# A graph layer's first tile: its products eight tiles behind x instead of six, three adjacency tiles requested later, and the first expert's weights requested behind x

## The chip, the cores and the metric

The kernel runs on one core of a Trainium2 chip. The metric is the device time of one execution in microseconds. Where several runs are shown, the median counts.

## What is computed

Two layers follow each other on x, 4096 tokens of 256 features, with adj a 4096 x 4096 adjacency of zeros and ones. The first is a graph convolution with residual, the second a mixture of 16 experts of which each token uses 2.

```python
deg = jnp.maximum((adj != 0).astype(jnp.float32).sum(-1), 1.0)
# graph layer on layernorm(x):
dinv = jax.lax.rsqrt(node_degree)
a_norm = dinv * (adjacency + jnp.eye(n)) * dinv
pooled = a_norm @ x + x
x = x_in + relu(pooled @ W + b)
# expert layer on layernorm(x), for e in range(16), top 2 of softmax(x @ Wr + br):
h = jax.nn.gelu(xf @ W1[e] + b1[e], approximate=False)
y = y + combine[:, e:e + 1] * (h @ W2[e] + b2[e])
x = x + xf + y
```

## The kernel before

Rows of x and of the adjacency are handled in 32 tiles of 128. The kernel has two halves.

**The graph half.** It does not compute a_norm @ x and then times W, but first y = layernorm(x) @ W for all 32 tiles of x and then the adjacency times y. y is kept in two float16 parts, a high half `yh` and a low half `yl` (inside the large buffer `wall`), so each product of an adjacency block with y is a pair of matmuls: L502 with the high half, L504 with the low half. An adjacency tile is 128 rows of the adjacency. It arrives as float16 in four quarters (`load_adj`, L255, into one of four slots of `abuf`), VectorE adds the identity (`add_own`, L876), transposes it in four chunks (`transpose_chunk`, L884) into `at`, and the TensorE products of a chunk wait for its transpose (`at_made`). An adjacency tile has 32 pairs, eight to a chunk.

The first stage, `first_tile` (L542 to L563), makes y and multiplies the first adjacency tile in the same loop. For each tile n of x:

- TensorE transposes x (`x_T`, L530) and multiplies tile n - 1 by W (`x_times_W`, L538). From n = LAG on, which is 6, it also multiplies adjacency block j = n - LAG (`neighbours`), after a wait for the chunk at every eighth j and for `y_low` of tile j. Ahead of the first of them stands one small product (L554). The loop runs until n = 32 + LAG - 1, so behind the last x times W come LAG pairs, of which the first stands in the same pass.
- ScalarE copies x transposed out of PSUM (`copy_x_T`, L749) and makes the high half of y (`high_y`, L756), scaled by the rstd of the token.
- VectorE makes the low half (`low_y`, L891) and the statistics of x six tiles ahead (`stats_of`, L844). When a group of tiles (`GROUPS`: 0-1, 2-4, 5-7, then four tiles each) is complete, five small instructions make its variance (L851 to L860). After the low half of tiles 4, 10, 18 and 26 (L907) it also transposes chunk 0, 1, 2 or 3 of adjacency tile 0, the first time after adding the identity.
- POOL makes rstd of each group (L1298), which waits for the variance. Behind groups 2, 4 and 6 it issues the four requests for adjacency tile 1, 2 or 3 (L1301). Those of tile 0 are issued earlier, from 5.57 us on.
- SP issues the requests for the larger part of x (L366 to L375), without waiting. ScalarE issues the others at the start.

Behind it `step` (L565 for TensorE, L395 for SP, L1047 for VectorE) runs for each adjacency tile t from 1 to 31, with what makes layer one's result, the router's choice and the rows for the experts, one and two tiles behind. SP's step 0 waits for the small `b2_cut` of VectorE, which comes when the x loop is over, then writes b2's low part, pads, and asks for the first matrix of expert 0 (L412, into `wst`); step 2 asks for the second one after it has stored a tile of the base. ScalarE (`cut_high_weights`, L694) and VectorE (`cut_low_weights`, L959) split them into two float16 parts. The weights of experts 1 to 7 follow in the loop in the same way, behind waits on `w_cut`.

**The expert half.** 79 blocks of 128 rows, each of one expert: transposes (L602), hidden products (L628), bias and gelu, transposes (L636), output products (L654), weighting, and an indirect DMA that adds the rows to the output (L1370). Between the halves stands a stretch in which the table of blocks is made.

The order on each engine is as written in the code. There is no scheduler.

Of the kernel before, what the change touches and what calls it, by code (L numbers as in the profile page):

```python
# [48 lines left out]
JC = CW // P  # L49
AB = 4  # L50
DEPTH = 2
LAG = 6
GROUPS = ((0, 2), (2, 5), (5, 8)) + tuple((n, n + 4) for n in range(8, 32, 4))
LEAD = 6
SG = 2.0 ** 8
# [11 lines left out]
XT = T // XC  # L67
# [20 lines left out]
def build(nc, x, adj, gnn_W, gnn_b, Wr, br, W1, b1, W2, b2, out):  # L88
# [5 lines left out]
    def sem(name):  # L94
        return ctx.enter_context(nc.semaphore(name))
# [119 lines left out]
    def ev(name):  # L215
        if name not in S:
            S[name] = sem(name)
        return S[name]

    def after(eng, name, t):  # L220

        eng.wait_ge(ev(name), t + 1)

    def passed(eng):


        eng.sem_inc(ev("passed"), 1)
# [5 lines left out]
    w_in = [sem(f"w_in{k}") for k in range(2)]  # L233
# [7 lines left out]
    def after_added(eng, q, r):  # L241

        n = q * (U // 2) + r // 2
        eng.wait_ge(added[r % 2], (n + 1) * 16)
# [8 lines left out]
    def load_adj(eng, i, k, b):  # L253

        eng.dma_start(arrived[b * PQ:(b + 1) * PQ, k % AB, :, :],  # L255
                      adj_v[bass.ds(pair(i, k), 1), k % 2, b, :, :, :].rearrange("n i a c -> i (n a) c"))\
           .then_inc(a_in[k % AB], 16)

    def load_x(eng, c, b):
        first, end = PIECES[c], PIECES[c + 1]  # L260
        eng.dma_start(xin[b * PQ:(b + 1) * PQ, first:end, :].rearrange("p (n h) d -> p n (h d)", h=2),
                      x_v[b][:, first // 2:end // 2, :]).then_inc(x_in[c], 16)
# [11 lines left out]
    def tile(i, k):  # L274

        return i * RUN + k

    def pair(i, k):

        return i * (RUN // 2) + k // 2  # L280
# [5 lines left out]
    def over_tiles(eng, step):  # L286

        for k in range(RUN):
            step(0, k)
        with eng.Fori(1, T // RUN - 1) as i:  # L290
            for k in range(RUN):
                step(i, k)
        for k in range(RUN + DEPTH):
            step(T // RUN - 1, k)

    def asked_at(i):

        return (0, 1) if isinstance(i, int) and i == T // RUN - 1 else (0, 2)
# [5 lines left out]
    def is_(t, cond):  # L304

        return cond(t) if isinstance(t, int) else True
# [16 lines left out]
    def w_dram(e, which):  # L323
        return (W1, W2)[which][bass.ds(e, 1), :, :].rearrange("a (c p) n -> p (a c) n", p=P)

    def staged(slot, which):
        return wst[:, slot, :].rearrange("p (c n) -> p c n", c=(DC, HC)[which])
# [10 lines left out]
    def fixed(q):  # L338

        return isinstance(q, int) and q == 0  # L340
# [21 lines left out]
    @block.sync  # L362
    def _(sp):
        sp.dma_start(wg_arrival, gnn_W.rearrange("(c p) n -> p c n", p=P)).then_inc(ev("w_gnn_in"), 16)
        for b in QUEUE[0]:
            load_x(sp, 0, b)  # L366
        for b in QUEUE[0]:
            load_x(sp, 1, b)
        for b in QUEUE[0]:
            load_x(sp, 2, b)  # L370
        for dst, src in consts:
            sp.dma_start(dst, src).then_inc(ev("consts_in"), 16)
        for c in (3, 4):
            for b in (0, 2, 1, 3):
                load_x(sp, c, b)  # L375

        def store_base(i, k):
            after(sp, "base_made", tile(i, k))
            sp.dma_start(out_v[bass.ds(pair(i, k), 1), k % 2, :, :, :].rearrange("n a i d -> (n a) i d"), base[k % 2])\
              .then_inc(base_out[k % 2], 16)  # L380

        def load_late(j):

            sp.wait_ge(ev("w_cut"), 2 * EARLY + (j - 1 if j >= 2 else 0))
            sp.dma_start(staged(j % 2, j % 2), w_dram(EARLY + j // 2, j % 2)).then_inc(w_late[j % 2], 16)

        b1_v = b1.rearrange("(c e) h -> c (e h)", c=CH).unsqueeze(1)

        def load_b1(c):

            sp.wait_ge(ev("at_made"), (T - AB + c + 1) * CH)
            n = E * H // CH
            sp.dma_start(b1all[:, c * n:(c + 1) * n], b1_v[c].broadcast_to([P, n])).then_inc(ev("b1_in"), 16)

        def step(i, k):  # L395
            t = tile(i, k)
            if is_(t, lambda t: 2 <= t < T + 2):
                store_base(i, k - 2)
            if isinstance(t, int) and T - 2 <= t < T:
                load_b1(t - T + 2)  # L400
            if isinstance(t, int) and t == 0:
                sp.wait_ge(ev("b2_cut"), 1)
                after(sp, "b2_zeros", 0)
                sp.dma_start(b2hl[E:2 * E, :], b2l).then_inc(ev("b2_in"), 16)
                after(sp, "pad_made", 0)
                sp.dma_start(rows[0:U * ROOM, :].rearrange("(e r) w -> r e w", r=ROOM)[0:P, :, :],
                             pad[:, :].unsqueeze(1).broadcast_to([P, U, RW])).then_inc(ev("first_pads"), 16)
            if k in asked_at(i):
                which = asked_at(i).index(k)
                if is_(i, lambda i: i >= 1):  # L410
                    sp.wait_ge(ev("w_cut"), i * 2 + which - 1)
                sp.dma_start(staged(which, which), w_dram(i, which)).then_inc(w_in[which], 16)  # L412
            if isinstance(t, int) and t == T - 1:
                load_late(0)
                load_late(1)

        over_tiles(sp, step)

        def load_block(q, r):
            if not isinstance(q, int) or q > 0:  # L420
                after_added(sp, q - 1, r)
            if fixed(q):
                row = r * ROOM
            else:
                passed(sp)
                row = sp.value_load(tab[0:1, bass.ds(in_table(q, r), 1)], min_val=0, max_val=PLACES - P)
            sp.dma_start(xg[r], rows[bass.ds(row, P), :]).then_inc(xg_in[r], 16)

        AHEAD = 4

        def bstep(q, r):
            nxt = shift(q, r, AHEAD)
            if is_block(nxt, 1, 0):
                after(sp, "table_made", 0)
                sp.wait_ge(ev("spare_pads"), 16)
                for which in range(len(PADS)):
                    after_pads(sp, which)
            if exists(*nxt):
                load_block(*nxt)
            if late(q, r) is not None and r % 2 and late(q, r) + 2 < 2 * (E - EARLY):  # L440
                load_late(late(q, r) + 2)

        for odd in (0, 1):
            sp.wait_ge(listed[odd], 16 * TOPK * T // 2)
        sp.wait_ge(ev("multiplied"), T * CH)
        for r in range(AHEAD):
            load_block(0, r)
        load_b1(2)
        load_b1(3)
        over_blocks(sp, bstep)  # L450


        for b in (BLOCKS - 2, BLOCKS - 1):
            after_added(sp, *divmod(b, U))
# [3 lines left out]
    def _(pe):  # L458
# [83 lines left out]
        def first_tile():  # L542

            for n in range(T + LAG):
                if n < T:
# [3 lines left out]
                if 0 <= n - 1 < T:  # L549
                    x_times_W(n - 1)  # L550
                j = n - LAG
                if j == 0:
# [279 lines left out]
    def _(dve):  # L832
# [45 lines left out]
        def transpose_chunk(i, k, c):  # L878

            n = tile(i, k) * CH + c  # L880
            after(V, "own_added", tile(i, k))
            if is_(n, lambda n: n >= CH):
                V.wait_ge(ev("multiplied"), n - CH + 1)
            V.transpose(at[:, c, :].bitcast(I32).rearrange("p (n a i) -> p a n i", a=Q, i=PQ),  # L884
                        arrived[:, k % AB, :, c * CW // CH:(c + 1) * CW // CH].bitcast(I32)
                        .rearrange("p a (n q) -> p a n q", q=PQ))\
             .then_inc(ev("at_made"), 1)
# [15 lines left out]
        for n in range(T):  # L903
            low_y(n)
            if n + LEAD < T:
                stats_up_to(n + LEAD)
            if n in (XT // 2, XT + 2, 2 * XT + 2, 3 * XT + 2):  # L907
                if n < XT:
                    add_own(0, 0)
                transpose_chunk(0, 0, n // XT)  # L910
            if n == T // 4 + 2:
                after(V, "gb_high", 0)
                V.scalar_tensor_tensor(out=gbm[P // 2:P, :], in0=gb[P // 2:P, :], scalar=SG, in1=gbm[P // 2:P, :],
                                       op0=ALU.mult, op1=ALU.subtract).then_inc(ev("gb_cut"), 1)
# [320 lines left out]
    def _(pool):  # L1235
        L = pool
# [63 lines left out]

        for g in range(len(GROUPS)):  # L1301
            rstd0(g)
            if g in (2, 4, 6):
                for b in range(Q):
                    load_adj(L, 0, g // 2, b)
        after(L, "pad_made", 0)
        L.dma_start(rows[E * ROOM:PLACES, :], pad[:, :]).then_inc(ev("spare_pads"), 16)
        L.wait_ge(ev("constants"), CONSTANTS)
# [101 lines left out]
```

## Time and profile before

| what | us |
|---|---|
| median of 3 runs | 627.83 |
| lowest and highest of them | 627.71, 632.73 |
| the profiled execution's own time | 626.15 |
| its span in the profile | 624.6 |
| TensorE busy | 582.1 (93%) |
| VectorE busy | 461.2 (74%) |
| POOL busy | 310.0 (50%) |
| ScalarE busy | 237.1 (38%) |

The profile follows one execution. All its rows are in microseconds from the start of the span. In a timeline row the first number is the start and the second the duration. The bracket at its end is the idle time of the engine just before it and what ended it. Durations of neighbouring matmuls overlap, as they are pipelined, so the time that one takes from the engine is the distance between two starts. In a row of the waits list the numbers are the total, how often, and the longest.

### The profile page before, as it was taken

The page shows a single profiled execution, that of the slowest core. Times are in us where ns is not written, and L with a number is a line of the kernel's source. Part 1 is how long each engine was busy: PE and PEld are TensorE (multiplying, and loading weights), DVE is VectorE, ACT ScalarE, POOL GpSimd, SP SyncE. Part 2 cuts the span into 40 slices and gives each one's busy share as a digit, 9 for nine tenths or more (in the row PEclk, how much of TensorE's full clock was granted, in tenths as well). Part 3 has the DMA queues.
Part 4 walks back from the last instruction along what each step waited for, and adds up shares of the span by engine and source line. Part 5 has one row for each costly group of instructions (what it writes and reads, how often), then busy time and mean ns, then how long its engine had stood idle before and what let it go on. Part 6 is the DMA issues. An engine that isn't in the chain of part 4 may idle for free. (4 is left out here: it accounts for less than half of the span.)

```text
span 624.6 us, 16840 instructions
## 1 busy us (share of the span) xinstructions
PE 582.1 (93%) x4756; PEld 461.0 (74%) x4756; DVE 461.2 (74%) x1469; ACT 237.1 (38%) x483; POOL 310.0 (50%) x361
## 2 busy tenths in 40 slices
PE   7899999999999999999839998999999999999992
PEld 6687888888888888888715665666677777777772
DVE  5777899999999999999855666666666666566561
ACT  3563443444444334344323444444432333323321
POOL 7333466666666666664342334525334443544343
PEclk9999999999999999999958999999999999999998
DMA  9976999999999999999548435766544543444430
GB/s 223 223 121 154 186 205 213 214 213 203 211 214 210 216 211 207 207 208 243 194 123 306 112 104 99 177 151 140 105 85 74 85 86 65 76 72 83 67 50 1
DMA packets 67605, 95.87 MB, mean 154 GB/s; under 512 B 9312, under 2 KB 42112, under 8 KB 67040
## 3 DMA queue, kind: packets, MB, share of 16 engines
q0 software_dynamic: 33408, 52.42, 48.4%
q1 hardware_dynamic: 32672, 40.88, 22.3%
q10 hardware_dynamic: 1472, 1.88, 0.9%
q8 instruction: 31, 0.51, 0.4%
q14 instruction: 22, 0.18, 0.1%
HBM read 103.71 MB, written 26.94 MB: 209 GB/s over the span
## 5 line engine op out<-in xcount | busy, mean ns | idle before, releaser
L502 PE MATMUL bank<-wall,at_xg 128*128 128x257 f16 x1024 | 238.8, 274 | 4.8 <-DVE at_xg L884 4.4
L504 PE MATMUL bank<-wall,at_xg 128*128 128x256 f16 x1024 | 233.6, 273 | 0.0
L1370 POOL DMA_INDIRECT out_dram<-orows,at_xg x79 | 123.9, 1568 | 161.7 <-DMA out_dram<-orows,at_xg 103.7
L1194 DVE SCALAR_TENSOR_TENSOR hl<-bank,xseT 128x512 f16<-128x512 f32 x79 | 54.6, 691 | 92.1 <-ACT xseT L817 92.1
L811 ACT ACTIVATE hgs<-hgs 128x512 f32<-128x512 f32 x79 | 49.8, 630 | 187.6 <-DVE hgs L1188 187.6
L628 PE MATMUL bank<-wall,feat 128*128 (+1 forms) x474 | 117.4, 385 | 2.1 <-DVE feat L1175 2.1
L502 PEld LDWEIGHTS bank<-wall,at_xg 128*128 128x128 f16 x1024 | 102.8, 100 | 21.6 <-DVE at_xg L884 8.2
L1338 POOL DMA_INDIRECT rows<-feat,posi x64 | 73.4, 1147 | 86.9 <-issue 82.2
L504 PEld LDWEIGHTS bank<-wall,at_xg 128*128 128x128 f16 x1024 | 100.2, 98 | 15.5 <-DVE wall L891 0.3
L654 PE MATMUL bank<-wall,xseT 128*128 (+1 forms) x632 | 108.2, 273 | 0.0
L884 DVE STREAM_TRANSPOSE at_xg<-abuf 128x512 int32<-128x512 int32 x128 | 87.0, 698 | 4.0 <-DVE abuf L876 0.3
L654 PE MATMUL bank<-wall,hl 128*128 (+1 forms) x316 | 86.2, 273 | 0.0
L628 PEld LDWEIGHTS bank<-wall,feat 128*128 128x128 f16 x474 | 46.3, 98 | 44.4 <-issue 7.3
L255 POOL DMA_DIRECT2D abuf<-in_adj_dram x128 | 74.1, 581 | 2.3 <-issue 1.3
L654 PEld LDWEIGHTS bank<-wall,xseT 128*128 128x128 f16 x632 | 61.6, 98 | 8.9
L1188 DVE SCALAR_TENSOR_TENSOR hgs<-bank,abuf 128x512 f32<-128x512 f32 x79 | 53.8, 680 | 0.1
L636 PE MATMUL bank<-id,hgs 128*128 128x128 f32 x316 | 47.9, 274 | 0.0
L817 ACT ACTIVATE xseT<-bank 128x512 f16<-128x512 f32 x79 | 45.7, 578 | 0.3 <-PE bank L636 0.3
L737 ACT ACTIVATE orows<-orows,bs 128x256 f32<-128x256 f32 x32 | 19.2, 601 | 66.8 <-DVE bs L972 66.8
L602 PEld LDWEIGHTS bank<-id,at_xg 128*128 128x128 f16 x316 | 24.1, 99 | 23.9 <-DMA at_xg<-rows 4.6
L1175 DVE COPY feat<-bank 128x512 f16<-128x512 f16 x79 | 33.3, 422 | 10.7 <-PE bank L602 8.2
L1202 DVE TENSOR_SCALAR orows<-bank,at_xg 128x256 f32<-128x256 f32 x79 | 37.5, 475 | 1.7 <-PE bank L654 1.7
(151 smaller groups left out, 765.0 us busy)
## 6 DMA issues: line engine op xcount, KB each, us to landing
abuf<-in_adj_dram POOLq DMA_DIRECT2D x128, 256.0 KB, 6.4
wst<-in_L_ffn_W_dram SPq DMA_DIRECT2D x32, 512.0 KB, 6.2
at_xg<-rows SPq DMA_DIRECT2D x79, 136.0 KB, 2.4
out_dram<-orows SPq DMA_DIRECT2D x32, 128.0 KB
abuf<-in_L_ffn_b_dram SPq DMA_DIRECT2D x4, 1024.0 KB, 8.2
wall<-in_x_dram SPq DMA_DIRECT2D x10, 256.0 KB, 12.8
rows<-pad POOLq DMA_DIRECT2D x11, 136.0 KB, 6.0
out_dram<-orows,at_xg POOLq DMA_INDIRECT x79
```

Source lines behind the costliest of these rows:

```text
L255: eng.dma_start(arrived[b * PQ:(b + 1) * PQ, k % AB, :, :], adj_v[bass.ds(pair(i, k), 1), k % 2, b, :, :, :].rearrange("n i a c -> i (n a) ...
L502: both = [lambda: pe.matmul(ps_acc[odd][:, 0:D + 1], w, yh[:, j, 0:D + 1], start=j == 0, stop=j == T - 1), lambda: pe.matmul(ps_acc[odd][: ...
L504: lambda: pe.matmul(ps_acc[odd][:, 0:D], w, yl[:, j, :], start=False, stop=False)]
L628: mm = pe.matmul(q_h[r % 2][:, :], a, w, start=n == 0, stop=n == 3 * DC - 1)
L636: mm = pe.transpose(q_g[r % 2][:, c * P:(c + 1) * P], hg[r % 2][:, c * P:(c + 1) * P], id32[:, :])
L654: mm = pe.matmul(q_o[r % 2][:, 0:D], a, w, start=False, stop=n == 3 * HC - 1)
L811: act.activation(hg[r % 2], hg[r % 2], ACT.Gelu).then_inc(ev("gelued"), 1)
L884: V.transpose(at[:, c, :].bitcast(I32).rearrange("p (n a i) -> p a n i", a=Q, i=PQ), arrived[:, k % AB, :, c * CW // CH:(c + 1) * CW // CH ...
L1188: V.scalar_tensor_tensor(out=hg[r % 2], in0=q_h[r % 2][:, :], scalar=1.0 / (SX * SW), in1=b1all[:, bass.ds(e * H, H)], op0=ALU.mult, op1=A ...
L1194: V.scalar_tensor_tensor(out=hl[:, r % 2, :], in0=q_g[r % 2][:, :], scalar=SH, in1=hh[:, r % 2, :], op0=ALU.mult, op1=ALU.subtract).then_i ...
L1338: L.indirect_dma_start(rows, at_place, feat[:, odd, k, :], None).then_inc(listed[odd], 16)
L1370: L.indirect_dma_start(out, bass.IndirectOffsetOnAxis(ap=info[r][:, 0:1].bitcast(U32), axis=0), orow[r], None, bounds_check=N - 1, oob_is_ ...
```

## The change

It has four edits.

1. LAG becomes 8: the products of adjacency tile 0 start two tiles of x later, and two more pairs are left behind the last x times W.
2. VectorE's four transposes of adjacency tile 0 move by two tiles, to behind the low halves of 6, 12, 20 and 28. The identity is added ahead of the first.
3. POOL asks for adjacency tiles 1, 2 and 3 behind groups 4, 6 and 7 of rstd instead of 2, 4 and 6.
4. SP asks for both matrices of expert 0 right behind its last request for x, instead of in steps 0 and 2.

```diff
-LAG = 6
+LAG = 8
+TURNS = (6, 12, 20, 28)
...
+        for which in range(2):
+            sp.dma_start(staged(which, which), w_dram(0, which)).then_inc(w_in[which], 16)
+
...
-            if k in asked_at(i):
+            if k in asked_at(i) and is_(i, lambda i: i >= 1):
                 which = asked_at(i).index(k)
-                if is_(i, lambda i: i >= 1):
-                    sp.wait_ge(ev("w_cut"), i * 2 + which - 1)
+                sp.wait_ge(ev("w_cut"), i * 2 + which - 1)
                 sp.dma_start(staged(which, which), w_dram(i, which)).then_inc(w_in[which], 16)
...
-            if n in (XT // 2, XT + 2, 2 * XT + 2, 3 * XT + 2):
-                if n < XT:
+            if n in TURNS:
+                if n == TURNS[0]:
                     add_own(0, 0)
-                transpose_chunk(0, 0, n // XT)
+                transpose_chunk(0, 0, TURNS.index(n))
...
-            if g in (2, 4, 6):
+            if g in (4, 6, 7):
                 for b in range(Q):
-                    load_adj(L, 0, g // 2, b)
+                    load_adj(L, 0, (4, 6, 7).index(g) + 1, b)
```

Line numbers of the changed kernel are one to three higher than those of the kernel before.

TensorE, around the first product of adjacency tile 0, before. `bank3`, `bank6` and `bank7` receive x times W of tiles 5, 6 and 7 here, `bank2` the adjacency's products.

```order
L530 MATMUL bank1<-id32,wall 128x128 x2
L538 MATMUL bank7<-orows,wall 128x256 x2
L530 MATMUL bank4<-id32,wall 128x128 x2
L538 MATMUL bank3<-orows,wall 128x256 x2
L554 MATMUL bank0<-firsts,ones16 128x16
L502 MATMUL bank2<-wall,at_xg 128x257
L504 MATMUL bank2<-wall,at_xg 128x256
```

The same place in the changed kernel:

```order
L533 MATMUL bank4<-id32,wall 128x128 x2
L541 MATMUL bank3<-orows,wall 128x256 x2
L533 MATMUL bank1<-id32,wall 128x128 x2
L541 MATMUL bank6<-orows,wall 128x256 x2
L533 MATMUL bank4<-id32,wall 128x128 x2
L541 MATMUL bank7<-orows,wall 128x256 x2
L557 MATMUL bank0<-firsts,ones16 128x16
L505 MATMUL bank2<-wall,at_xg 128x257
L507 MATMUL bank2<-wall,at_xg 128x256
```

Two transposes of x and two products with W (tiles 6 and 7) now stand ahead of the small product and of the wait for the first chunk.

VectorE, around the first transposed chunk, before. `bank6`, `bank7` and `bank3` give the low halves of tiles 3, 4 and 5.

```order
L891 SCALAR_TENSOR_TENSOR wall<-bank6,rstd,wall 128x256
L844 BN_STATS st6<-wall 128x6
L891 SCALAR_TENSOR_TENSOR wall<-bank7,rstd,wall 128x256
L844 BN_STATS st6<-wall 128x6
L876 TENSOR_TENSOR abuf<-abuf,own_col 128x4x64
L884 STREAM_TRANSPOSE at_xg<-abuf 128x4x4x32
L891 SCALAR_TENSOR_TENSOR wall<-bank3,rstd,wall 128x256
```

The same place in the changed kernel:

```order
L894 SCALAR_TENSOR_TENSOR wall<-bank7,rstd,wall 128x256
L847 BN_STATS st6<-wall 128x6
L894 SCALAR_TENSOR_TENSOR wall<-bank3,rstd,wall 128x256
L847 BN_STATS st6<-wall 128x6
L854 TENSOR_TENSOR dif<-st6 128x4
L855 TENSOR_TENSOR var<-st6 128x4
L857 TENSOR_TENSOR dif<-dif 128x4
L859 TENSOR_SCALAR var<-var 128x4
L863 SCALAR_TENSOR_TENSOR var<-dif,var 128x4
L894 SCALAR_TENSOR_TENSOR wall<-bank6,rstd,wall 128x256
L847 BN_STATS st6<-wall 128x6
L879 TENSOR_TENSOR abuf<-abuf,own_col 128x4x64
```

The low halves of tiles 5 and 6, their statistics and the variance of group 3 now come ahead of the identity, with the transpose right behind it.

## Rows read from the trace of the kernel before

**Rows 1.** The page's slices (40 of equal length): TensorE's busy tenths and granted clock.

```profile
PE   7899999999999999999839998999999999999992
...
PEclk9999999999999999999958999999999999999998
```

**Rows 2.** Windows: busy time of PE, PEld, DVE, ACT, POOL, clock, DMA share, GB/s.

```profile
62.00:70.00 8.00, 8.00 (x76) 7.10 (x75) 6.61 (x26) 3.51 (x7) 2.26 (x5) 1.00 1.03 196
...
100.00:300.00 200.00, 199.63 (x1836) 175.25 (x1835) 184.41 (x750) 81.02 (x185) 122.38 (x163) 1.00 1.01 210
```

**Rows 3.** Timeline of PE, 15 to 20 us, around the first product.

```profile
15.20 0.38 PE L530 MATMUL bank<-id,wall 128*128 128x128 f32 x2
...
16.29 0.17 PE L554 MATMUL bank<-firsts,ones 128*128 128x16 f16 x1
19.31 0.29 PE L502 MATMUL bank<-wall,at_xg 128*128 128x257 f16 x1 [2.85 <-DVE at_xg L884]
```

**Rows 4.** Timelines of DVE and ACT in the x loop, 15 to 28 us.

```profile
15.91 0.48 DVE L891 SCALAR_TENSOR_TENSOR wall<-bank,rstd,wall 128x256 f16<-128x256 f32 x1 [0.26 <-ACT wall L756]
...
16.55 0.47 ACT L756 ACTIVATE wall<-bank,rstd 128x256 f16<-128x256 f32 x1 [0.40 <-PE bank L538]
...
18.21 0.30 DVE L876 TENSOR_TENSOR abuf<-abuf,own_col 128x256 f16<-128x256 f16 x1 [1.48 <-DMA abuf<-in_adj_dram]
...
25.25 0.48 DVE L891 SCALAR_TENSOR_TENSOR wall<-bank,rstd,wall 128x256 f16<-128x256 f32 x1 [0.42 <-ACT wall L756]
...
26.74 0.48 DVE L891 SCALAR_TENSOR_TENSOR wall<-bank,rstd,wall 128x256 f16<-128x256 f32 x1
...
27.47 0.69 DVE L884 STREAM_TRANSPOSE at_xg<-abuf 128x512 int32<-128x512 int32 x1
```

**Rows 5.** Timeline of PE, 52 to 57 us, the end of the stage.

```profile
52.49 1.03 PE L538 MATMUL bank<-orows,wall 128*128 128x256 f32 x4
...
53.58 0.27 PE L502 MATMUL bank<-wall,at_xg 128*128 128x257 f16 x1
...
53.80 0.27 PE L502 MATMUL bank<-wall,at_xg 128*128 128x257 f16 x1
...
56.56 0.28 PE L502 MATMUL bank<-wall,at_xg 128*128 128x257 f16 x1 [1.56 <-DVE at_xg L884]
```

**Rows 6.** Timeline of DVE: the identity of adjacency tiles 1 and 3.

```profile
55.48 0.28 DVE L876 TENSOR_TENSOR abuf<-abuf,own_col 128x256 f16<-128x256 f16 x1
...
70.42 0.28 DVE L876 TENSOR_TENSOR abuf<-abuf,own_col 128x256 f16<-128x256 f16 x1
```

**Rows 7.** Timeline of POOL: requests for tiles 0 and 2, rstd of group 7.

```profile
5.57 2.46 POOL L255 DMA_DIRECT2D abuf<-in_adj_dram  x4
...
27.89 2.20 POOL L255 DMA_DIRECT2D abuf<-in_adj_dram  x4
...
42.89 1.02 POOL L1298 TENSOR_TENSOR rstd<-var,mhalf 128x4 f32<-128x4 f32 x1 [2.04 <-DVE var L860]
```

**Rows 8.** DMA issues at 14.9-17.3 and 27.5-30.5 us; the adjacency's landings, 0 to 80.

```profile
abuf<-in_adj_dram POOLq DMA_DIRECT2D x4, 256.0 KB, 11.0
...
abuf<-in_adj_dram POOLq DMA_DIRECT2D x4, 256.0 KB, 5.6
...
DMA to landing us min/median/max: 4.4/6.0/13.5
```

**Rows 9.** Timelines of SP's queue and of ACT: x's last requests, the first weights' cut.

```profile
7.36 7.27 SPq L261 DMA_DIRECT2D wall<-in_x_dram  x8
...
62.95 1.05 ACT L694 ACTIVATE wall<-wst 128x1024 f16<-128x1024 f32 x1
```

**Rows 10.** A window, and the timeline of PE, where the expert half begins.

```profile
332.00:334.00 2.00, 1.56 (x12) 0.89 (x11) 1.20 (x3) 0.77 (x1) 0.54 (x1) 0.92 1.01 416
...
330.55 2.32 PE L628 MATMUL bank<-wall,feat 128*128 128x512 f16 x6 [0.61 <-DVE feat L1175]
...
337.86 1.46 PE L628 MATMUL bank<-wall,feat 128*128 128x512 f16 x6
...
341.24 1.46 PE L628 MATMUL bank<-wall,feat 128*128 128x512 f16 x6
```

## The prediction

> **What bounds the kernel now.** I read the page's slices first. TensorE is the engine to watch: its busy digit is 9 in nearly every slice, except in the first, around the middle and at the end, and its granted clock is 1.00 nearly everywhere [rows 1]. So every edit here is worth what it takes from TensorE's waits in the first 60 us, unless it disturbs something later. The table of windows confirms this: from 100 to 300 us TensorE is busy 199.63 of 200 us [rows 2]. A transfer or a VectorE step that comes earlier there can win at most 0.4 us.
>
> Next I read TensorE's timeline of the first stage. One pass of the loop over x (two transposes of L530, four L538 passes of x times W) takes 1.09 us (15.20 to 16.29). After the seventh pass and the small L554 product, TensorE stands still for 2.85 us, until 19.31, waiting for the first transposed chunk of adjacency tile 0 [rows 3]. VectorE's timeline tells why: it issues the low half of y of tile 4 at 15.91, one statistics instruction follows, then it waits 1.48 us for the adjacency's transfer (the waits list names it), adds the identity at 18.21 and transposes behind it; 1.10 us after 18.21 TensorE runs [rows 3, 4]. So there are two causes in a row: a transfer that landed at about 18.2, and VectorE reaching that point about one pass late in any case.
>
> The third place is the end of the stage. The last x times W starts at 52.49, and TensorE waits 1.56 us before 56.56 for the first chunk of adjacency tile 1, so the products of tile 0 end at 55.00 [rows 5]. VectorE gets there only after the low half of y of tile 31, some small steps and the addition at 55.48 [rows 6]. The distance from the last x times W to the first product of tile 1 is 56.56 - 52.49 = 4.07 us. It is a chain through ScalarE and VectorE, and the tile's own transfer was asked for at 14.9 to 17.3 [rows 8], long before.
>
> **Part 1, products eight tiles behind x, and the transposes two tiles later.** No instruction is added or removed. TensorE does passes 7 and 8 before its first wait: 16.29 + 2 x 1.09 = 18.47, and with L554's 0.17 it is ready at 18.64. VectorE now does two more low halves, two more statistics and one group's variance ahead of the identity. ScalarE starts the high half of y of tile 5 at 16.55 and ends it at 17.02 [rows 4], so VectorE's low half of tile 5 can start at about 17.07; before, it stood behind the wait for the transfer. From one low half to the next with a variance between them takes 1.49 us (25.25 to 26.74), and from a low half over a statistics instruction to what follows 0.73 us (26.74 to 27.47) [rows 4]. That puts the low half of tile 6 at 18.56 and the identity at 19.29, 1.1 us after the transfer has landed. From the identity's start to the first product took 19.31 - 18.21 = 1.10 us, so the product starts at 20.39. TensorE's wait is 20.39 - 18.64 = 1.75 us instead of 2.85: a gain of 1.10 us. What is late next is VectorE itself, no more the transfer.
>
> Bounds of this term. If VectorE were never late, all 2.85 us would go. On the other side, the slowest adjacency quarter of the first 80 us landed 13.5 us after its request [rows 8]. The last quarter of tile 0 is asked for at about 7.5 (POOL issues the four from 5.57 on, 2.46 us in all [rows 7]); landing at 21.0 would put the product at 22.1 and the wait at 3.5 us, 0.6 us more than before. I take 1.10, since each step of it has a row close by.
>
> At the stage's end two pairs of products more are left after the last x times W. One pair takes 0.22 us (53.58 to 53.80), two 0.44 us [rows 5]. The chain of 4.07 us through ScalarE and VectorE has the same instructions as before, and TensorE has 0.44 us more to do beside it: the wait of 1.56 becomes 1.12. Bounds: 0 if some other instruction is in the way, and 1.56 if the chain also became shorter; nothing makes it so.
>
> In between, the loop is bound by TensorE (no wait between 19.31 and 55.00), and every transpose keeps its distance of three passes to the product that needs it, as both moved by two. So nothing is gained or lost there.
>
> **Part 2, adjacency tiles 1 to 3 asked for later on POOL's queue.** The requests go from behind variance groups 2, 4, 6 to behind 4, 6, 7. Each tile's four requests take 2.2 us of POOL, and with one tile's requests just ahead of it POOL still stood idle 2.04 us before the rstd of group 7, so no rstd becomes late. The x loop runs 1.10 + 0.44 = 1.54 us ahead of its old times. So tile 1 is asked for at 27.89 - 1.5 = 26.4 and tile 3 at 42.89 + 1.02 - 1.5 = 42.4 [rows 7], tile 2 a group of four passes (some 5 us) ahead of that, at 37.1. Quarters asked for at 27.9 landed in 5.6 us at the median [rows 8]. Even if the last request goes out 2.2 us after the first and takes the 13.5 us of the slowest, tile 1 is there at 42.1, tile 2 at 52.8 and tile 3 at 58.1. Tile 1's identity is due at 55.48 - 1.5 = 54.0, tile 2's later than that, tile 3's at 70.42 - 1.5 = 68.9 [rows 6]. The cost is zero, with 10 us of cover for tiles 1 and 3. It would show as a wait of VectorE at L879 of the changed kernel.
>
> **Part 3, the first expert's weights asked for behind x on SP's queue.** Two requests of 512 KB leave the stretch 56 to 72 us and take the place behind x that tile 1's requests had on the other queue: 1 MB against 1 MB. SP issues its last x request by 14.63 (7.36 + 7.27) [rows 9] and then only waits for the end of the stage, so it may block there. The weights were read first by ScalarE's cut at 62.95 [rows 9], without idle time before it, and TensorE was busy through 62 to 70 us (8.00 of 8.00) [rows 2]. So earlier weights win nothing: 0, at most the 0.4 us of TensorE's idle time from 100 to 300 us through less crowded transfers. As a loss: were they to crowd x or adjacency tile 0, it comes under the bound of part 1.
>
> A row and a rule stand against that zero. Adjacency quarters asked for at 14.9 to 17.3, beside x, took 11.0 us, those asked for alone 5.6 [rows 8]: transfers asked for by different engines slow each other. The Trainium skill, in "DMA: Bandwidth & Descriptors", section "Queues, rings and completion order", says that each DMA engine takes turns between the queues that have work and reads one queue's ring in order. By its first half alone the weights would slow tile 0; by its second half they stand behind x, and tile 0 shares with one queue, as before. Where weights and x were fetched side by side after all, three streams instead of two would stretch what is left of tile 0 after about 15 us.
>
> **The sum.** -1.10 - 0.44 = -1.54 us. The profiled execution took 626.15 us (its span is 624.6), so it would take 624.6. The median of the runs shown is 627.83, 1.7 above that execution; on it the forecast is 626.3 us, 0.24% less. A change of under 1% is about what a measurement of this kernel cannot tell from none, and this is far inside it.
>
> **Rivals.**
> *A, adjacency tile 0 lands later.* What is left of it from 15.0 to 18.2 is stretched by 1.5 (three streams for two): 3.2 becomes 4.8, landing at 19.8. VectorE is ready at 19.29, so the product comes 0.5 us later and the gain is 1.0: 626.8 us. With the slowest landing it is a loss of 0.6 against the 0.44 at the end, thus 628.0. For it: the 11.0 against 5.6. Against it: the weights are requested only after the last x load, at 14.6. Chance 0.10, at about 627.
>
> *B, the change moves waits only.* VectorE's longer queue ahead of the first transpose (1.49 us from one low half to the next) makes TensorE wait as long as before, two passes later, and the end of the stage is held by VectorE too: 627.8 us. For it: VectorE is the engine named in both waits. Against it: its work before the transpose fits into time in which it stood waiting. Chance 0.05.
>
> *C, more is won.* VectorE's part is shorter than worked out, the first wait falls to near 0.5 us, and the lighter traffic after 56 us gives the 0.4 more: -3.2 us, 624.6. For it: nothing else stands between TensorE and the chunk. Against it: the rows that I summed are from the same loop. Chance 0.09.
>
> *D, slower: the clock comes back later in the middle.* Between the two halves TensorE is at the lower of its two levels, 0.50 (1.2 GHz) [rows 1]; it returns to 1.00 (2.4 GHz) in the window 332 to 334, whose mean is 0.92 [rows 10]. Six L628 products took 2.32 us while it was mostly at the low level and 1.46 at the high one, and a whole block takes 3.38 us there (337.86 to 341.24) [rows 10]. A shift by 1.5 us leaves the work of that stretch as it was, but if the clock rose one block later, that block would lose between the 0.9 us of its L628 alone and 3.4, if all of it took twice as long. I take 3, since TensorE hardly waits in a block: less the 1.54 won, 629.3. It decides once the rise is over 3 us later. For it: the level is low just where the expert stage begins. Against it: what TensorE does before the rise is the same, only earlier. Chance 0.05. To lose 1% the rise would have to come over 15 us later, as a lower clock costs at most half of the time it lasts.
>
> The forecast itself keeps 0.71. By these cases the result is within 1% in all but rare ones: 0.02 faster by over 1%, 0.96 within, 0.02 slower. The range of eight in ten runs from C's 624.6 to a bit past rival A's worst case, 628.4; the likeliest case's own range is 625.5 to 627.2.
>
> **What would show it.** In the changed profile TensorE's wait before the first product should be 1.8 us, starting at about 18.6, and VectorE should have no wait for the adjacency at the first identity. The wait before tile 1 should be 1.1 us, and tile 1's first product at about 55.0 instead of 56.56. POOL's requests stand at about 26, 37 and 42 us, with no wait of VectorE for any of them. The weights land before 35 us and TensorE's busy time between 62 and 300 us stays as it was. The hidden product that stood at 330.55 and the clock's rise should both come 1.5 us earlier [rows 10]. The prediction is wrong if a wait for x appears in the x loop, if the identity waits for its transfer, if a later adjacency tile is late, or if the middle stretch changes its length.

## The result, and the profile after

| | before | changed |
|---|---|---|
| median | 628.49 us of 9 runs (627.71 to 632.73) | 624.89 us of 9 runs (624.34 to 627.39) |
| the profiled execution's own time | 626.15 | 624.49 |
| its span | 624.6 | 623.0 |

The ratio is 0.9936 with a 95% interval of [0.9918, 0.9953]: 3.6 us less, by the interval 3.0 to 5.2. Forecast were 1.5 us less. So the direction was right, and the gain is more than twice as large. Between the two profiled executions alone it is 1.66 us, close to the 1.54 of the sum. The gap lies between the profiled execution of before (626.15) and the kernel's usual execution (628.49 at the median); the changed kernel's profiled execution (624.49) is close to its own median.

First the profile after, at the places of the sum. TensorE's timeline of the first stage (start, duration, what, and in the bracket the idle time before it and what ended it):

```profile
16.28 0.38 PE L533 MATMUL bank<-id,wall 128*128 128x128 f32 x2
...
18.45 0.17 PE L557 MATMUL bank<-firsts,ones 128*128 128x16 f16 x1
20.35 0.28 PE L505 MATMUL bank<-wall,at_xg 128*128 128x257 f16 x1 [1.72 <-DVE at_xg L887]
...
50.92 1.03 PE L541 MATMUL bank<-orows,wall 128*128 128x256 f32 x4
...
54.99 0.29 PE L505 MATMUL bank<-wall,at_xg 128*128 128x257 f16 x1 [1.26 <-DVE at_xg L887]
```

These answer to [rows 3] and [rows 5]. TensorE is ready at 18.6, the product starts at 20.35 (forecast 20.39) after 1.72 us of waiting (1.75), and tile 1 begins at 54.99 instead of 56.56 (forecast 55.0). VectorE's timeline of the same stretch, beside [rows 4]:

```profile
17.05 0.48 DVE L894 SCALAR_TENSOR_TENSOR wall<-bank,rstd,wall 128x256 f16<-128x256 f32 x1 [0.33 <-ACT wall L759]
...
18.54 0.48 DVE L894 SCALAR_TENSOR_TENSOR wall<-bank,rstd,wall 128x256 f16<-128x256 f32 x1
...
19.27 0.28 DVE L879 TENSOR_TENSOR abuf<-abuf,own_col 128x256 f16<-128x256 f16 x1
```

The identity at 19.27 has no bracket: VectorE no longer waits for the adjacency's transfer. The low halves stand at 17.05 and 18.54, where the sum had 17.07 and 18.56. POOL's requests for tiles 1 to 3 and the landings, beside [rows 7] and [rows 8]:

```profile
26.29 2.23 POOL L256 DMA_DIRECT2D abuf<-in_adj_dram  x4
...
37.08 2.21 POOL L256 DMA_DIRECT2D abuf<-in_adj_dram  x4
...
42.38 2.19 POOL L256 DMA_DIRECT2D abuf<-in_adj_dram  x4
```

```profile
DMA to landing us min/median/max: 4.2/6.0/11.2
```

Nobody waits for any of these tiles. The first expert's weights are requested at 14.4 and 14.9 us and take 12.7 and 13.9 us, so they are there before 29 us. Their first cut on ScalarE follows its predecessor without a gap as before, 1.57 us earlier than the 62.95 of [rows 9], and from 100 to 300 us TensorE is busy for the same 199.63 us as in [rows 2]:

```profile
61.38 1.05 ACT L697 ACTIVATE wall<-wst 128x1024 f16<-128x1024 f32 x1
```

```profile
100.00:300.00 200.00, 199.63 (x1839) 175.50 (x1838) 184.43 (x746) 82.11 (x186) 122.20 (x163) 1.00 1.01 211
```

### The profile page after: what moved, and what is told of

Its sections match the earlier page's. It is cut to its first block and busy times, and to the rows that moved or that the text cites. A ratio compares the mean times of both kernels' runs of the same rounds, so it can differ in the third digit from the quotient of the medians.

```text
span 623.0 us, 16840 instructions
## 1 busy us (share of the span) xinstructions
PE 582.5 (94%) x4756; PEld 462.4 (74%) x4756; DVE 460.7 (74%) x1469; ACT 236.9 (38%) x483; POOL 309.6 (50%) x361
```

## The experiments

Three theories stood at the start. By the first, adjacency tile 0 lands at a time that differs between executions, usually later than in the one profiled. By the second, the extra time of before is lost in the traffic after 56 us. By the third, the profiled execution was lucky here and there over its whole length. Unless another kernel is named, ratios are to the kernel before, measured on the same chip in the same job.

**The kernel before once more.** No edit.

> The kernel before, unchanged, for a second profile and more times. Theory 1 (the first adjacency tile lands at a time that differs between executions, and in the usual execution later than the 18.2 us of the profile at hand): ratio 1.000 to itself; if the new profiled execution takes 628 us or more, its identity waits longer than 1.48 us, with the identity at about 20 us. Theory 2 (the usual execution loses its two extra microseconds after 56 us, where weights, pads and adjacency are fetched together, or in the expert half): the identity stands at 18.2 as before and the extra time shows up later. Theory 3 (the profiled execution of before was no more than a lucky one, by differences spread over the whole): small differences everywhere.

Measured: 629.01 us at the median of 12 runs, ratio 1.000 [0.9981, 1.0018]. The profiled execution took 628.91 us, 2.8 more than the one that the prediction used. Its timelines of TensorE and VectorE:

```profile
20.74 0.35 PE L502 MATMUL bank<-wall,at_xg 128*128 128x257 f16 x1 [4.28 <-DVE at_xg L884]
...
60.56 0.27 PE L463 MATMUL bank<-gbm,gb_ones 128*128 128x256 f16 x1
```

```profile
19.64 0.29 DVE L876 TENSOR_TENSOR abuf<-abuf,own_col 128x256 f16<-128x256 f16 x1 [2.91 <-DMA abuf<-in_adj_dram]
```

The identity waits 2.91 us instead of 1.48 and TensorE 4.28 instead of 2.85: a landing 1.43 us later. But tile 1's own product (L463, 0.90 us behind the tile's first product) stands 3.10 us later than in the first profile:

```profile
57.46 0.27 PE L463 MATMUL bank<-gbm,gb_ones 128*128 128x256 f16 x1
```

The windows (length, granted clock, DMA share, GB/s) of the second profile show where the other 1.67 us are:

```profile
18.00:20.00 2.00, 1.00 1.07 251
20.00:22.00 2.00, 0.71 1.09 247
22.00:24.00 2.00, 0.50 1.11 253
24.00:26.00 2.00, 0.94 1.12 249
26.00:28.00 2.00, 1.00 1.08 200
```

After standing still for 4.28 us TensorE has the lower level (0.50, 1.2 GHz) until about 24 us. In the first profile it waited 2.85 us and kept 1.00 in each of these windows. The Trainium skill ("TensorE: Matmul & The Clock Gate", section "HAM oscillation — how this bites in real kernels") describes a matmul kernel whose waits for transfers throttle the clock again and again. This trace agrees as far as a single wait can: 4.28 us of it, and then the level 0.50.

**Edits 1 and 2 alone.**

```diff
-LAG = 6
+LAG = 8
+TURNS = (6, 12, 20, 28)
```

> Edits 1 and 2 alone (LAG 8 and the transposes two tiles later). Theory 1: nearly the whole gain, 3.0 to 3.6 us less than before (ratio about 0.995), as the landing now has 1.1 us of cover. Theory 2: 1.5 us less, ratio 0.9976. Theory 3: 1.5 us less.

Measured: 625.83 us (12 runs), ratio 0.9951 [0.9932, 0.9971], 3.3 us less on medians. The first product stands at 20.38 after a wait of 1.73 us, the clock is 1.00 from 18 to 34 us, tile 1 starts at 55.02, and the span is 622.8. That is the whole of the changed kernel's gain as far as the intervals can tell. The 0.9976 of the second and the third theory lies just outside.

```profile
20.38 0.28 PE L503 MATMUL bank<-wall,at_xg 128*128 128x257 f16 x1 [1.73 <-DVE at_xg L885]
...
55.02 0.28 PE L503 MATMUL bank<-wall,at_xg 128*128 128x257 f16 x1 [1.26 <-DVE at_xg L885]
```

**Edit 3 alone.**

```diff
-            if g in (2, 4, 6):
+            if g in (4, 6, 7):
```

> Edit 3 alone (adjacency tiles 1 to 3 requested behind groups 4, 6, 7, LAG 6). Theory 1: 0, or up to 2 us less if it is tile 1's requests at 14.9 us that hold up the end of tile 0's transfer; then the identity stands clearly before 18.2. Theory 2: 0 or slightly slower, as adjacency moves towards the crowded stretch. Theory 3: 0.

Measured: 629.38 us (12 runs), ratio 1.0010 [0.9989, 1.0031]: nothing. In its profile the identity stands at 18.89 although tile 1's requests are no longer there at 14.9, so in this execution they are not what holds up tile 0. TensorE's wait and the clock behind it:

```profile
20.00 0.40 PE L502 MATMUL bank<-wall,at_xg 128*128 128x257 f16 x1 [3.52 <-DVE at_xg L884]
```

```profile
18.00:20.00 2.00, 0.78 1.06 278
20.00:22.00 2.00, 0.50 1.06 284
22.00:24.00 2.00, 0.50 0.67 191
24.00:26.00 2.00, 0.51 0.00 0
```

Here the low level lasted until 26 us, and tile 1's own product stands at 61.04, 3.58 us later than in the first profile, of which the landing explains 0.68.

**Edit 4 alone.**

```diff
+        for which in range(2):
+            sp.dma_start(staged(which, which), w_dram(0, which)).then_inc(w_in[which], 16)
```

> Edit 4 alone (the first expert's weights requested behind x, LAG 6, adjacency as before). Theory 1: 0 to 1 us slower, since tile 0, x, tile 1 and the weights are then in flight together. Theory 2: 2 us less (ratio 0.997), since 1 MB leaves the stretch 56 to 72 us. Theory 3: 0.

Measured: 628.96 us (12 runs), ratio 0.9984 [0.9956, 1.0012]: no difference that can be told from zero. The 2 us less of the second theory lie inside this interval, so this run alone does not exclude them. What speaks against them is that edits 1 and 2 without this one have the whole gain. The identity stands at 18.97, TensorE waits 3.59 us, the clock reads 0.76 and 0.50 in the windows from 20 to 24, and tile 1's own product is at 59.91.

So there are four profiles of LAG 6 with tile 0 requested at its usual place, the first among them, with the identity at 18.21, 18.89, 18.97 and 19.64. In three of them the clock falls. Only the one that the prediction used escaped. Two of the four are of the kernel before itself; the other two carry edit 3 or edit 4. How the landing is spread over the timed runs, which have no profile, is not known.

**Work in the wait.**

```diff
+                    if j == 0:
+                        for _ in range(10):
+                            pe.matmul(ps_mean[:, 0:P], one_dth, one_dth, start=True, stop=True)
                     if j % JC == 0:
                         pe.wait_ge(ev("at_made"), j // JC + 1)
```

> The kernel before with ten extra 128x128 float32 products (into a PSUM bank that nobody reads then) between the small product L554 and TensorE's wait for the first chunk of adjacency tile 0. They change no data and take some 2 us in which TensorE would stand still. Theory clock (in the usual execution tile 0 lands at 19 to 19.6 us, TensorE's wait of 3.5 to 4.3 us is followed by a stretch at granted clock 0.50, and that stretch costs 1.2 to 2 us on top of the wait): the remaining wait is at most 2.2 us, the clock stays 1.00 from 18 to 28 us, and the median is 1.2 to 2 us under before although TensorE starts its first product no earlier. Rival (the wait alone is the cost): the same time as before, or slower by what the extra products overrun.

Measured: 628.43 us (12 runs) against 629.21, ratio 1.0000 [0.9981, 1.0020]. The profile does what the clock theory says. The landing was as late as in the second profile of before, the extra products took the idle time, and the clock stayed:

```profile
16.34 2.48 PE L558 MATMUL bank<-wall 128*128 128x128 f32 x20
20.72 0.28 PE L502 MATMUL bank<-wall,at_xg 128*128 128x257 f16 x1 [1.90 <-DVE at_xg L887]
```

```profile
20.00:22.00 2.00, 1.00 1.11 241
22.00:24.00 2.00, 1.00 1.08 234
```

The first product starts 0.02 us from its place in that profile, 20.74, but tile 1's own product is at 58.87 instead of 60.56: 1.69 us is the price of the clock's fall in the first stage. At the end of the program only 0.7 us of it is left (span 626.6 against 627.3), and the medians differ by 0.8 us, which is not clear of zero. In the ten profiles of this study without late requests the time from tile 1's own product to the end of the span varies between 566.2 and 567.9 us, so a single pair cannot show more. The forecast of 1.2 to 2 us at the median is not borne out: the interval's lower end, 0.9981, allows 1.2 us at most.

One more number on record bears on this, the mean granted clock of each execution. Over the 12 runs with edits 1 and 2 alone it is 0.9794 on average, over the 35 of the kernel before in that job 0.9759. With the work in the wait it is 0.9785, against 0.9767. Worked out from these and the level 0.50, an estimate: the kernel before spends some 4.4 and 2.2 us more of an execution at the lower level. That has the sign of the clock theory, but it does not say where. The middle has such a stretch of its own, and the first two profiles of before both read 0.979, the one without and the one with a fall in the first stage.

**LAG 10, with the transposes of the change.**

```diff
-LAG = 8
+LAG = 10
```

> The changed kernel with LAG 10, transposes still behind tiles 6, 12, 20, 28. By the sum of the prediction: TensorE is ready for the first product at 18.45 + 2 x 1.09 = 20.6 us, the chunk is made at 20.3, so the wait of 1.7 us goes; two more pairs at the end leave 0.8 of the 1.26 us before tile 1. Together 2.1 us less than the changed kernel, 622.8 at the median, and a narrower spread, since a landing as late as 19.6 costs nothing any more. Rival (x or VectorE becomes the bound once TensorE no longer waits): less than 1 us gained.

Measured: 622.59 us (6 runs, 621.38 to 624.17), ratio 0.9902 [0.9875, 0.9930]. TensorE has no wait before the first product at all, and the one before tile 1 is as worked out:

```profile
19.32 0.28 DVE L879 TENSOR_TENSOR abuf<-abuf,own_col 128x256 f16<-128x256 f16 x1
```

```profile
52.82 0.28 PE L505 MATMUL bank<-wall,at_xg 128*128 128x257 f16 x1 [0.81 <-DVE at_xg L887]
```

Tile 1 starts 2.17 us before its place in the changed kernel. The forecast of 622.8 came. I read this as follows, and did not test it: the same sum that was too small for the change holds here, since in both profiles VectorE's identity stands behind the landing (19.27 and 19.32, without a bracket).

**LAG 14.**

```diff
-LAG = 8
+LAG = 14
```

> The changed kernel with LAG 14, transposes still behind tiles 6, 12, 20, 28. By the sum: no wait before the first product and, with 14 pairs of 0.22 us behind the last x times W, 0 us of the 1.26 before tile 1: 3.0 us less than the changed kernel, 621.9 at the median. Rival: with 1.09 us per pass and no products in between, VectorE or the x transfer holds the loop at passes 9 to 16, and the gain is no larger than that of LAG 10.

Measured: 622.27 us (6 runs, 621.55 to 625.38), ratio 0.9905 [0.9876, 0.9933]. The last wait is gone too: tile 1's own product stands at 52.83, with LAG 10 at 53.73. TensorE has no wait from 13 to 60 us in this profile, so the rival's mechanism, a loop held by VectorE or by x, is not there. But its number came, a gain no larger than that of LAG 10: the end of the program does not show the 0.9 us (span 620.1 against 620.2), and the intervals cannot tell the two versions apart. Where the 0.9 us go stays open.

**Tile 0's requests 4 us earlier, LAG 6.**

```diff
         L = pool

+        for b in range(Q):
+            load_adj(L, 0, 0, b)
```

> The kernel before (LAG 6) with tile 0's four adjacency requests as POOL's first instructions, 4 us earlier. Theory landing: tile 0 lands before 17 us, the identity stands at 16.8 without a wait for a transfer, the first product at 17.9, TensorE waits 1.45 us and the clock stays 1.00: 3 to 4 us less than before at the median, unless the early x comes later by about as much. Rival (the landing is not what makes the usual execution long): 1.4 us less at the most.

Measured: 629.03 us (12 runs), ratio 1.0000 [0.9982, 1.0018]. A miss. The identity does not wait for its tile any more, but it stands at 20.32 where 16.8 was expected, because x comes later:

```profile
8.58 0.63 PE L530 MATMUL bank<-id,wall 128*128 128x128 f32 x4 [1.49 <-DMA wall<-in_x_dram]
...
12.54 0.69 PE L530 MATMUL bank<-id,wall 128*128 128x128 f32 x2 [1.09 <-DMA wall<-in_x_dram]
...
21.40 0.28 PE L502 MATMUL bank<-wall,at_xg 128*128 128x257 f16 x1 [1.26 <-DVE at_xg L884]
```

The two transfers are fetched side by side, and what one gains the other loses: TensorE's transposes that wait for x stand at 8.58 and 12.54 where the first profile has 6.13 and 9.38. The clock was at 0.50 from 10 to 16 us in this execution. It fell after 9 us, behind the waits of 1.49 and 0.35 us for x; the one of 1.09 us came later. The small product ahead of the adjacency (L554) is 3.67 us late, 19.96 against 16.29, and how much of that is x and how much the clock is not separated.

**Tile 0's requests later, with LAG 6, 8 and 10.** The same block of four requests stands behind POOL's constants in all four. The second of them adds the extra products of the fill kernel with `range(20)`.

```diff
-        for b in range(Q):
-            load_adj(L, 0, 0, b)
...
+        for b in range(Q):
+            load_adj(L, 0, 0, b)
+
         def rstd0(g):
```

> The kernel before (LAG 6) with tile 0's four adjacency requests moved behind POOL's constants, 2.4 us later (8.0 instead of 5.6 us). Theory landing and clock: the identity stands 1 to 2.4 us later than in the usual execution, at 20.5 to 22; TensorE waits 5 to 6 us, the granted clock falls to 0.50 in every execution, and the median is 1 to 3 us over before. Rival (the landing is hidden or of no account): the same time as before.

> e8 with twenty extra products in TensorE's wait (4.9 us by the 2.48 us that ten took). The landing is that of e8. Theory landing and clock: the clock stays 1.00 and the time is 1.2 to 2 us under e8. Rival (the wait alone costs): the time of e8, or more if the extra products overrun.

> The changed kernel (LAG 8) with tile 0's requests 2.4 us later. Theory landing and clock: TensorE is ready at 18.6 and the product starts at 21.5 to 23, a wait of 3 to 4.5 us in which the clock falls; the cover of the change is used up, and the time is 2 to 4 us over the changed kernel, about 627 to 628.

> e5 (LAG 10) with tile 0's requests 2.4 us later. Theory landing and clock: TensorE is ready at 20.6, the wait is 1 to 2.2 us, the clock stays 1.00, and the time is 1 to 2 us over e5, about 624. Rival (the gain of a longer lag has nothing to do with the landing): the same distance to e10 as e5 has to the changed kernel, 2.3 us, whatever the clock does.

| kernel | median us (runs) | ratio to before | identity at | TensorE's wait | tile 1's first product |
|---|---|---|---|---|---|
| late, LAG 6 | 636.06 (6) | 1.0112 [1.0071, 1.0153] | 25.64 | 9.75 | 65.97 |
| late, LAG 6, twenty products | 635.95 (6) | 1.0097 [1.0067, 1.0128] | 25.49 | 3.35 | 65.52 |
| late, LAG 8 | 633.97 (12) | 1.0059 [1.0031, 1.0086] | 25.51 | 7.43 | 63.88 |
| late, LAG 10 | 631.81 (12) | 1.0020 [0.9995, 1.0045] | 25.88 | 5.50 | 61.44 |

All four missed the size. The second gave the number of its rival, the time of the first, and LAG 10 the number of its own, the same distance to LAG 8 as with the usual requests (2.2 against 2.3 us). I had put the landing as much later as the requests. POOL issued them 3.0 us later, not 2.4, and the identity moved by 6.0 to 7.4 us, to 25.6:

```profile
8.57 2.42 POOL L255 DMA_DIRECT2D abuf<-in_adj_dram  x4 [0.44 <-issue]
```

```profile
25.64 0.29 DVE L876 TENSOR_TENSOR abuf<-abuf,own_col 128x256 f16<-128x256 f16 x1 [8.38 <-DMA abuf<-in_adj_dram]
```

In all four the clock fell, so they don't separate it from the wait. The twenty products don't either. They left a wait of 3.35 us, after which the window 28 to 30 reads 0.50 again, and in that execution the clock had already dropped in the x loop, to 0.71 in the window 12 to 16. Ahead of that stood this wait, the longest since 8 us:

```profile
12.60 1.13 PE L538 MATMUL bank<-orows,wall 128*128 128x256 f32 x4 [1.94 <-ACT wall L752]
```

What these runs do show is the value of the lag when the landing is late. From LAG 6 to 8 tile 1 starts 2.09 us earlier and from 8 to 10 another 2.44, and the medians fall by 2.1 and 2.2 us. Two passes over x are 2.17 us of work (16.28 to 18.45 in the changed kernel), and nearly all of it comes off the wait, which falls by 2.32 and 1.93. So a landing that is 6 us later does not make the step from LAG 6 to 8 worth more: it gave 3.6 us with the usual requests and 2.1 here, where the clock falls with either lag.

## Why the prediction was wrong

**Term by term, for the profiled execution, it was right.** The first wait's gain was 1.13 us (2.85 to 1.72) where the sum had 1.10. The wait at the end of the stage fell by 0.30 where it had 0.44: the chain from the last x times W to tile 1's product is 4.07 us in both (50.92 to 54.99), but TensorE's wait in it is 1.26 and not 1.12. Tile 1 starts 1.57 us earlier where the sum had 1.54, since the last pass itself comes 1.57 us earlier. For edits 3 and 4 the sum had nothing, and alone neither is clear of zero (1.0010 and 0.9984); together they were not run without the other two, but with them the gain (0.9936) is not to be told from that of edits 1 and 2 alone (0.9951).

**The step that failed is the sum, with its term of 1.10 us for the first wait: worked out for the profiled execution, which "would take 624.6", it was then set on the median.** I noted that the profiled execution lay 1.7 us under the median of the runs, and carried the difference over as if it were the same for both kernels. It is for the larger part a difference that the change removes. (With nine runs the median of before is 628.49 and the difference 2.3 us.) The bound had named the cause, "the slowest adjacency quarter", but I used it only against the change: a landing later than 18.2 was priced as a loss of the changed kernel, up to 0.6 us. The kernel before pays for each such microsecond in full, and the changed one only from about 19.3 on. And the sum had no term for the clock behind that wait.

Worked out again for the usual execution, with the second profile of before: the first wait is 4.28 us. With a landing like that (identity at 19.64) the changed kernel's product would start at 20.7 instead of 20.35, so its wait is 2.1, and the gain is 2.2. The stage's end gives 0.3, and the clock, which no longer falls, 1.7 by the pair of profiles with the same landing. Together 4.2 us. With the landing of edit 3's profile (18.89) the first wait gives 3.52 - 1.72 = 1.8, so that even with the smallest price of the clock the sum is 3.8. With that profile's own price of the clock, 2.9, it would be 5.0. The measured 3.6 us (3.0 to 5.2) fit all three. Without the clock the two landings give 2.1 and 2.5 us, less than was measured, so the landing as seen in these profiles is not enough. How much of the gain is the clock at the median stays open. The work in the wait shows its 1.69 us where the stage ends, but only 0.8 us, not clear of zero, in the medians, and the late requests didn't isolate it. With the 1.2 us that its interval allows at most, the sums for the two landings are 3.7 and 3.3.

**Second failed step: the clock was looked for in the wrong place.** Rival D placed it in the middle, where a level of 0.50 showed in the page. In the first stage the profile read 1.00 throughout, after a wait of 2.85 us, and the prediction prices no fall there. In the middle nothing was lost: its first blocks stood 1.6 to 1.7 us earlier, and the rise came in the window 328 to 330 (0.89) instead of 332 to 334 [rows 10], some 4 us earlier where 1.5 had been forecast. TensorE's timeline of the changed kernel there. The second row, at 328.90, answers to the one at 330.55 that took 2.32 us before:

```profile
325.15 2.72 PE L631 MATMUL bank<-wall,feat 128*128 128x512 f16 x6 [0.70 <-DVE feat L1178]
...
328.90 1.46 PE L631 MATMUL bank<-wall,feat 128*128 128x512 f16 x6 [0.61 <-DVE feat L1178]
...
332.26 1.45 PE L631 MATMUL bank<-wall,feat 128*128 128x512 f16 x6 [1.24 <-DVE feat L1178]
...
336.15 1.46 PE L631 MATMUL bank<-wall,feat 128*128 128x512 f16 x6
```

TensorE wins 0.86 us on the second block and waits 1.24 us for VectorE before the third, so that the fourth is again where a plain shift puts it (336.15, before 337.86).

Of the rivals, A and B did not come. C, "more is won", named the right sign with the wrong cause: neither a shorter VectorE part nor the traffic after 56 us. The first wait is 1.72 us, not its 0.5, so that its 624.6 stands so close to the measured 624.89 is luck.

A faster version came out of this: the changed kernel with LAG 10 takes 622.59 us at the median, 0.98% less than before. It is 2.3 us less than the changed kernel took, but the two were not measured side by side, and their intervals against before overlap (0.9875 to 0.9930, and 0.9918 to 0.9953).

## What to carry to other kernels

A profile is one execution. Where its own time lies below every timed run, as 626.15 did below 627.71, ask which of its waits was short by luck before any number is taken from it; a wait that ends with a transfer in crowded traffic is the first candidate, and here one second profile of the same kernel showed it. A change that puts work in front of such a wait gains by how late the transfer usually is, but no more than the work that it moves, here 2.2 us. Where the clock fell behind the wait and no longer does, the stage also gets back the slow stretch (1.69 us in the pair of profiles with the same landing).

## What the runs showed that was not expected

- The same program has its first adjacency tile ready at 18.2 us in one execution and 19.6 in another.
- In the first stage TensorE's clock stayed at 1.00 behind waits of 1.72, 1.90 and 2.85 us and was at 0.50 soon after waits of 3.35, 3.52, 3.59 and 4.28 us. The length of the last wait alone does not decide it: earlier in the x loop the clock also fell soon after waits of 1.94 us (late requests with twenty products) and of 1.49 and 0.35 us (early requests). After the waits of 3.52 and 4.28 us the slow stretch cost 1.7 to 2.9 us up to tile 1 (3.10 - 1.43, and 3.58 - 0.68).
- A transfer requested 3.0 us later while x is being fetched was ready 6.0 to 7.4 us later, and one requested 4 us earlier left the median where it was (629.03 against 629.21), since x came later.
